# Where the short chunk of keys stands in a streamed cross attention: last instead of first

## Chip, core and metric

One Trainium2 core of one chip runs the whole program in one launch. The metric is the device time of that launch in microseconds (us); lower is better.

## The reference, cut to what matters

The program computes two layers of a Perceiver-like network on 128 queries of width 256, with a context of 12544 rows of width 256. The change touches the first block alone, a softmax attention of 16 heads (key width 64, value width 16) from the queries to the context:

```
q = layernorm(x) @ wq            # 128 x 1024, 16 heads of 64
k = ctx @ wk;  v = ctx @ wv      # 12544 x 1024, 12544 x 256
x = x + softmax(q k^T / 8) v     # per head, over all 12544 keys
```

The softmax runs over chunks of keys with a running maximum, so the result doesn't depend on the order of the chunks. A small attention, a gated feed-forward net, a second cross attention, another attention and a mixture of experts follow. They are not changed and wait for the first block's sum.

## The kernel before, in words

12544 keys are 24 chunks of 512 and one of 256 (`CHUNK_TILES` = 4 tiles of 128 keys, `TAIL_TILES` = 2). Two buffers ("slots") alternate for everything that a chunk owns. The five engines' programs are written out by hand and meet at semaphores; each engine works strictly in its own order.

A chunk has eight **steps** t, each with 32 queries of 8 heads. For a step TensorE (PE) forms scores (`scores`, L383), VectorE (DVE) takes the extreme over the keys (`maxima`, L604), ScalarE (ACT) takes exponentials from the score banks (`exponentials`, L541, two per step), and DVE transposes them (`turn_probabilities`, L623). Two pairs of score banks alternate, so PE's scores of step t+2 wait for ACT to have read step t (`scores_read`).

Between the scores PE makes the **keys of the next chunk** (`next_keys`, L360: 8 head pairs p, six matmuls each, since fp32 is split into high and low fp32r parts), this chunk's **values** (L367) and the sum **weighted** by the previous chunk's probabilities (L393). ACT copies the keys out (`keep_keys`, L531), some between the two exponentials of a step.

What depends on the running maximum goes a longer way. After step 7 ACT writes the factor `x_shrink` (L556, signal `alpha_ready`), SP places it per head with 16 small DMAs (`place_by_head`, L818), and GpSimd (POOL) then runs, in this order, `rescale` (L766 to L772), `set_aside` (L783, which prepares `vals`, the stationary side of the weighted sum, and signals `vals_ready`), `split_context` (L749) and `add_out` (L755, L758).

At the beginning the ACT queue loads the first chunk's context and then `wk` and `wv`; the SP queue loads `x`, `wq` and the second chunk's context at the same time. Before the first step there are the queries (L375), the split of `wk` into high (ACT, L568, L573) and low (DVE, L708) parts, and all eight key groups of the first chunk. At the end, `last_chunk` has no keys of a next chunk to make. It does the weighted sum of the chunk before in four quarters at t = 0 to 3, and its own in two parts: head quads (0, 1) after the scores of step 7 and once `vals_ready` is there, quads (2, 3) after the last transposition and after `acc_whole`, with small reordering matmuls (L449) between. Then come `outputs` and the next block.

Before, the order is 256, 512, ..., 512. Each full chunk's keys are always made in the chunk before.

Of the kernel before, what the change touches and what calls it, by code (L numbers as in the profile page):

```python
# [335 lines left out]
KEEP_BETWEEN, KEEP_AFTER = {0: 5, 4: 0}, {1: (6, 7), 5: (1, 2), 6: (3,), 7: (4,)}  # L336


def step_after(slot, t, nt, ahead, by=1):

    if t + by < STEPS:
        return slot, t + by, nt
    return (1 - slot, t + by - STEPS, CHUNK_TILES) if ahead else None


LAST_HALF, LAST_SUM = 3, 4
# [7 lines left out]
def xattn0_tensor(pe, m, s, n):  # L354
# [54 lines left out]
    def next_keys(slot, p, ahead):  # L409

        if p < 2:
            values_turned()
        if p == 0:
            pe.wait_ge(s["ctx_split"], n("ctx_split", 2))
            if ahead > 1:
                pe.sem_inc(s["raw_free"], 1)
        if p >= 2 and p != 5:
            pe.wait_ge(s["k_kept"], n("k_kept"))
        for i in range(TERMS):
            done = key_term(1 - slot, p, CHUNK_TILES, 4 + p % 2, i)  # L420
# [74 lines left out]
    for half in range(2):  # L495
        queries(half)
        if half == 0:
            pe.wait_ge(s["ctx_split"], n("ctx_split", 2))
            pe.sem_inc(s["raw_free"], 1)
        pe.wait_ge(s["wk_split"], n("wk_split"))  # L500
        for p in range(4 * half, 4 * half + 4):
            if p % 4 >= 2:
                pe.wait_ge(s["k_kept"], n("k_kept"))
            for i in range(TERMS):
                done = key_term(0, p, TAIL_TILES, 4 + p % 2, i)
            done.then_inc(s["k_full"], 1)
        pe.wait_ge(s["q_ready"], n("q_ready"))
        if half == 0:
            pe.wait_ge(s["k_kept"], n("k_kept", 2))
            for t in range(2):  # L510
                scores(0, t, TAIL_TILES)
    pe.wait_ge(s["wv_split"], n("wv_split"))
    chunk(0, TAIL_TILES, 0, 2)
    chunk(1, CHUNK_TILES, TAIL_TILES, 2)
    for _ in range((N_FULL - 4) // 2):
        chunk(0, CHUNK_TILES, CHUNK_TILES, 2)
        chunk(1, CHUNK_TILES, CHUNK_TILES, 2)
    chunk(0, CHUNK_TILES, CHUNK_TILES, 2)
    chunk(1, CHUNK_TILES, CHUNK_TILES, 1)
    last_chunk(0, CHUNK_TILES, CHUNK_TILES)  # L520


def xattn0_scalar(act, m, s, n):
    def split_context(slot, k, nt):
        if k == 0:
            act.wait_ge(s[f"raw{slot}"], n(f"raw{slot}", 16))
        act.copy(m.c_hi[slot][:, k, 0:nt * P], m.raw[slot][:, k, 0:nt * P]).then_inc(s["ctx_hi"], 1)  # L527

    def keep_keys(slot, p, nt):
        act.wait_ge(s["k_full"], n("k_full"))  # L530
        act.copy(m.keys[slot][:, p, 0:nt * P], m.bank(4 + p % 2)[:, 0:nt * P]).then_inc(s["k_kept"], 1)  # L531

    def keep_queries(half):
        act.wait_ge(s["q_full"], n("q_full"))
        act.mul(m.qT[:, 4 * half:4 * half + 4, :], m.bank(6 + half).rearrange("p (h c) -> p h c", c=P),
                -float(X0_DK) ** -0.5).then_inc(s["q_ready"], 1)

    def exponentials(slot, t, nt, between=None):
        act.wait_ge(s["max_ready"], n("max_ready"))
        for odd in range(2):  # L540
            i = act.activation(m.probs[t % 2][:, odd, 0:nt * P], m.ps[:, 2 * (t % 2) + odd, 0:nt * P], ACT.Exp,  # L541
                               bias=m.peak[slot][:, 1, 2 * (t // 4) + odd, t % 4:t % 4 + 1], scale=-1.0,
                               accum_out=m.totals[slot][:, 1, 2 * (t // 4) + odd, t % 4:t % 4 + 1])
            if odd == 0 and between:
                keep_keys(*between, CHUNK_TILES)
        i.then_inc(s["probs_ready"], 1)
        act.drain().then_inc(s["scores_read"], 1)  # L547

    def chunk(slot, nt, ahead, first=False):
        for t in range(2 if first else 0, STEPS):  # L550
            keys = 1 - slot if t > 1 else slot
            kept = t < 2 or ahead
            exponentials(slot, t, nt, (keys, KEEP_BETWEEN[t]) if kept and t in KEEP_BETWEEN else None)
            if t == STEPS - 1:
                act.wait_ge(s["below_ready"], n("below_ready"))
                act.activation(m.shrink[slot][:, :, :, :], m.below[:, :, :, :],  # L556
                               ACT.Exp).then_inc(s["alpha_ready" if ahead else "alpha_last"], 1)
            if kept:
                for p in KEEP_AFTER.get(t, ()):
                    keep_keys(keys, p, CHUNK_TILES)  # L560
            if ahead > 1 and t in SPLIT_STEPS:
                split_context(slot, SPLIT_STEPS.index(t), CHUNK_TILES)

    for k in range(DK):
        split_context(0, k, TAIL_TILES)
    layer_norm_scalar(act, m, s, n, 3)
    act.wait_ge(s["wk0"], 16)
# [25 lines left out]
    chunk(0, CHUNK_TILES, 2)  # L593
    chunk(1, CHUNK_TILES, 1)
    chunk(0, CHUNK_TILES, 0)
    act.wait_ge(s["last_full"], 1)
    act.copy(m.last_out[:, :, :], m.ps[:, 6:8, 0:P]).then_inc(s["last_kept"], 1)


def xattn0_vector(dv, m, s, n):  # L600
# [112 lines left out]
    maxima(0, 0, TAIL_TILES)  # L713
    chunk(0, TAIL_TILES, 0, 2)
    chunk(1, CHUNK_TILES, 1, 2)
    chunk(0, CHUNK_TILES, 2, 2)
    chunk(1, CHUNK_TILES, 2, 2)
# [5 lines left out]
        n.restart(dv, s, *looped)  # L723
    chunk(0, CHUNK_TILES, 2, 2)
    chunk(1, CHUNK_TILES, 2, 1)
    last_chunk(0, CHUNK_TILES)
    outputs()


def xattn0_pool_init(gp, m, s, n):  # L730
    for k in range(DK):
        gp.wait_ge(s["ctx_hi"], n("ctx_hi"))
        gp.tensor_tensor(m.c_lo[0][:, k, 0:TAIL], m.raw[0][:, k, 0:TAIL], m.c_hi[0][:, k, 0:TAIL],
                         ALU.subtract).then_inc(s["ctx_split"], 1)
    gp.memset(m.peak[0][:, 0, :, :], 3e38)
    gp.memset(m.totals[0][:, 0, :, :], 0.0)
# [9 lines left out]
def xattn0_pool(gp, m, s, n):  # L746
# [74 lines left out]
def xattn0_sync(sp, m, s, n, a):  # L821
# [973 lines left out]
```

## Time and profile before

| | us |
|---|---|
| median of 3 runs (lowest, highest) | 983.76 (981.04, 983.9) |
| the profiled execution: its own time | 983.17 |
| its span in the trace | 981.4 |
| PE busy in the span | 950.7 (97%) |
| end of the first cross attention in the span | about 657 |

The trace gives each instruction's start and duration. A matmul's recorded duration holds its latency, so the pace of a stream is read from the starts, or from the chain of waits, which gives a stretch and the number of instructions in it. A plain fp32 matmul of the program is recorded as two instructions: the eight score matmuls of one step are "x16". The program's line numbers in the rows are those of the listing above.

### The profile page before, as it was taken

Reading aid. Unit: us, or ns where it says so; the run is one execution under the profiler, and the core shown is the slowest. Engines: PE = TensorE matmul, PEld = TensorE weight load, DVE = VectorE, ACT = ScalarE, POOL = GpSimd, SP = SyncE. Lnnn points to the kernel's source line nnn. Section 1 sums busy time; section 2 is a strip of 40 time slices with the busy share of each in tenths; the row PEclk is TensorE's granted clock in tenths of the full one; section 3 lists DMA queues with packets and bytes.
Section 4 is the critical chain, followed back from the end, with each engine's and each line's share of the span. In section 5 each row is a group of like instructions: output and inputs, shape, how many; then the busy total and the mean of one; then the engine's idle time right before and its main releaser. Section 6 shows DMA issues by size and latency. Waiting matters only on the chain.

```text
span 981.4 us, 30783 instructions
## 1 busy us (share of the span) xinstructions
PE 950.7 (97%) x13281; PEld 702.9 (72%) x13281; DVE 692.2 (71%) x871; ACT 587.1 (60%) x1404; POOL 368.3 (38%) x405
## 2 busy tenths in 40 slices
PE   6999999999999999999999999988989999899998
PEld 6666666666666666666666666668977787789998
DVE  3788888888888888888888888763025555467886
ACT  5677766666666667666666666622236663336664
POOL 2344444444444444444444343330013333213332
PEclk9999999999999999999999999998999999999999
DMA  6010101000000000000100000049538888508993
GB/s 220 25 25 24 24 24 24 25 24 24 25 24 24 25 24 25 24 24 24 25 24 24 25 3 3 4 186 390 182 149 264 276 279 286 173 1 277 325 336 97
DMA packets 78295, 97.80 MB, mean 100 GB/s; under 512 B 21584, under 2 KB 56672, under 8 KB 78176
## 3 DMA queue, kind: packets, MB, share of 16 engines
q1 hardware_dynamic: 77088, 94.40, 29.7%
q8 instruction: 104, 1.70, 0.7%
q10 hardware_dynamic: 1088, 1.57, 0.4%
q14 instruction: 15, 0.12, 0.0%
HBM read 95.42 MB, written 0.13 MB: 97 GB/s over the span
## 4 chain that ended last, share of the span: by engine, by line
PE 89%; issue 4%; DVE 3%; POOL 2%; DMA 2%; ACT 1%; SPq 0%; ACTq 0%; DVEq 0%; POOLq 0%
PE ps L360 29%; PE ps L383 18%; PE ps L393 10%; PE ps L367 7%; PE ps L1493 6%; PE ps L1098 3%; PE ps L997 3%; PE ps L1510 2%; PE ps L1514 2%; PE ps L1511 2%; PE ps L1087 1%; PE ps L1089 1%; POOL m_w_lo L1475 1%; PE ps L1088 1%; DMA m_shared_w<-in_m_sw 1%
## 5 line engine op out<-in xcount | busy, mean ns | idle before, releaser
L541 ACT ACTIVATE probs<-ps,x_peak 128x512 f32<-128x512 f32 (+1 forms) x400 | 269.5, 678 | 178.1 <-DVE x_peak L604 167.4
L604 DVE TENSOR_REDUCE x_peak<-ps 128x2 f32<-128x1024 f32 (+1 forms) x200 | 237.0, 1185 | 93.7 <-PE ps L383 93.7
L623 DVE STREAM_TRANSPOSE probsT<-probs 128x1024 f32<-128x1024 f32 (+1 forms) x200 | 242.9, 1215 | 13.2 <-ACT probs L541 12.7
L383 PE MATMUL ps<-keys,qT 64*32 64x512 f32 (+1 forms) x3200 | 195.7, 584 | 2.5 <-ACTq L547 1.6
L360 PE MATMUL ps<-ctxT_hi,wk_hi 128*128 128x512 f32 (+1 forms) x400 | 163.2, 408 | 0.8 <-ACT keys L531 0.8
L360 PE MATMUL ps<-ctxT_lo,wk_hi 128*128 128x512 f32 (+1 forms) x400 | 155.2, 388 | 0.0
L783 POOL TENSOR_SCALAR vals<-vals_t,x_side 128x512 f32<-128x512 f32 (+1 forms) x100 | 152.2, 1541 | 7.6 <-PEq L407 3.9
L360 PE MATMUL ps<-ctxT_hi,wk_lo 128*128 128x512 f32 (+1 forms) x400 | 154.2, 386 | 0.0
L360 PEld LDWEIGHTS ps<-ctxT_hi,wk_hi 128*128 128x128 f32 x400 | 75.6, 189 | 73.7 <-issue 39.8
L531 ACT COPY keys<-ps 128x512 f32<-128x512 f32 (+1 forms) x200 | 110.4, 577 | 28.7 <-PE ps L360 20.8
L749 POOL TENSOR_TENSOR ctxT_lo<-ctx_raw,ctxT_hi 128x512 fp32r<-128x512 f32 x48 | 61.6, 1284 | 133.4 <-ACT ctxT_hi L527 133.4
L383 PEld LDWEIGHTS ps<-keys,qT 64*32 64x32 f32 x3200 | 58.7, 106 | 70.6 <-issue 52.5
L393 PE MATMUL ps<-probsT,vals 64*32 64x128 f32 x6272 | 104.2, 271 | 1.4 <-DVE probsT L623 1.4
L393 PEld LDWEIGHTS ps<-probsT,vals 64*32 64x32 f32 x6272 | 90.5, 105 | 19.7 <-issue 19.6
L360 PEld LDWEIGHTS ps<-ctxT_hi,wk_lo 128*128 128x128 f32 x400 | 75.6, 189 | 15.7
L360 PEld LDWEIGHTS ps<-ctxT_lo,wk_hi 128*128 128x128 f32 x400 | 75.8, 189 | 12.2
L541 ACT ACTIVATION_READ_ACCUMULATOR probs<-ps,x_peak 128x1 f32 x400 | 78.5, 196 | 0.0
L1279 POOL TENSOR_TENSOR c1T_lo<-ctx_two,c1T_hi 128x512 fp32r<-128x512 f32 (+1 forms) x25 | 31.3, 1251 | 103.7 <-ACT c1T_hi L1160 103.7
L766 POOL TENSOR_TENSOR x_parts<-x_totals,x_shrink 128x32 f32<-128x32 f32 x24 | 6.1, 253 | 159.5 <-DMA x_shrinkT<-x_shrink 159.5
L1465 POOL TENSOR_TENSOR m_w_lo<-m_w,m_w_hi 128x1024 fp32r<-128x1024 f32 x15 | 35.5, 2364 | 72.0 <-ACT m_w_hi L1542 72.0
L1493 PE MATMUL ps<-xnT,m_w 128*128 128x128 f32 x512 | 59.9, 275 | 0.0
L1493 PEld LDWEIGHTS ps<-xnT,m_w 128*128 128x128 f32 x512 | 58.6, 192 | 0.3 <-issue 0.3
(252 smaller groups left out, 1302.3 us busy)
## 6 DMA issues: line engine op xcount, KB each, us to landing
m_w<-in_m_w SPq DMA_DIRECT2D x32, 1024.0 KB, 7.7
ctx_raw<-in_ctxT SPq DMA_DIRECT2D x24, 512.0 KB, 3.7
ctx_two<-in_ctxT SPq DMA_DIRECT2D x24, 512.0 KB, 4.3
ctx_one<-in_ctx SPq DMA_DIRECT2D x24, 512.0 KB, 5.6
x_shrinkT<-x_shrink SPq DMA_DIRECT2D x384, 1.0 KB, 1.7
f_h1T<-in_f_h1T SPq DMA_DIRECT2D x1, 4096.0 KB, 18.2
f_h2T<-in_f_h2T SPq DMA_DIRECT2D x1, 4096.0 KB, 27.9
m_shared_w<-in_m_sw SPq DMA_DIRECT2D x2, 1024.0 KB, 7.9
```

The source lines that it names most:

```text
L360: return pe.matmul(m.bank(bank)[:, 0:nt * P], w[:, k, p * P:(p + 1) * P], c[:, k, 0:nt * P], start=(i == 0), stop=(i == TERMS - 1))
L367: return pe.matmul(m.bank(4 + half)[:, 0:nt * P], w[:, k, half * P:(half + 1) * P], c[:, k, 0:nt * P], start=(i == 0), stop=(i == TERMS - 1))
L383: i = pe.matmul(m.ps[32 * j:32 * (j + 1), 2 * (t % 2) + odd, 0:nt * P], m.qT[rows, 4 * group + j, qs], m.keys[slot][rows, 4 * group + j, 0 ...
L393: i = pe.matmul(m.ps[32 * c:32 * (c + 1), 6 + two, 0:P], m.vals[slot][rows, b, c, :], m.probsT[slot][rows, c, b, :], start=(b == 0), stop= ...
L531: act.copy(m.keys[slot][:, p, 0:nt * P], m.bank(4 + p % 2)[:, 0:nt * P]).then_inc(s["k_kept"], 1)
L541: i = act.activation(m.probs[t % 2][:, odd, 0:nt * P], m.ps[:, 2 * (t % 2) + odd, 0:nt * P], ACT.Exp, bias=m.peak[slot][:, 1, 2 * (t // 4) ...
L604: dv.tensor_reduce(m.peak[slot][:, 1, cs, t % 4], m.ps[:, 2 * (t % 2):2 * (t % 2) + 2, 0:nt * P], AX.X, ALU.min).then_inc(s["dve" if t == ...
L623: i = dv.transpose(m.probsT[slot][:, cs, 0:4 * nt, t % 4 * 32:t % 4 * 32 + 32], m.probs[t % 2][:, :, 0:nt * P].rearrange("p c (b k) -> p c ...
L749: gp.tensor_tensor(m.c_lo[slot][:, k, 0:nt * P], m.raw[slot][:, k, 0:nt * P], m.c_hi[slot][:, k, 0:nt * P], ALU.subtract).then_inc(s["ctx_ ...
L783: t = gp.tensor_scalar(m.vals[slot][:, 0:4 * nt, cs, side * X0_DV:(side + 1) * X0_DV], m.vals_t[slot][:, 0:4 * nt, cs, :], m.side[:, side: ...
L1465: eng.tensor_tensor(m.w2_lo[c % 2][:, os, :], second_weights(m, c)[:, os, :], m.w2_hi[c % 2][:, os, :], ALU.subtract).then_inc(s[f"m_w2_lo ...
L1493: t = pe.matmul(m.bank(2 * (c % 2) + half)[:, i * P:(i + 1) * P], w1[:, k, o * P:(o + 1) * P], m.xnT[:, k, :], start=(k == 0), stop=(k == ...
```

## The change

The tail of 256 keys becomes the last chunk and the first chunk has 512 keys. The tail's context is still the first 256 columns of the array; only the time of its turn changes. `following(ahead)` gives the size of the chunk whose keys are made ahead (256 when one chunk is left), and `third` the size of the context that is split two chunks ahead. Counts of instructions don't change on PE, DVE, ACT and POOL; the shapes at both ends do. The core of the diff:

```diff
+def following(ahead):
+    return TAIL_TILES if ahead == 1 else CHUNK_TILES
...
-            done = key_term(1 - slot, p, CHUNK_TILES, 4 + p % 2, i)
+            done = key_term(1 - slot, p, following(ahead), 4 + p % 2, i)
...
-                done = key_term(0, p, TAIL_TILES, 4 + p % 2, i)
+                done = key_term(0, p, CHUNK_TILES, 4 + p % 2, i)
...
-                scores(0, t, TAIL_TILES)
+                scores(0, t, CHUNK_TILES)
...
-    chunk(0, TAIL_TILES, 0, 2)
-    chunk(1, CHUNK_TILES, TAIL_TILES, 2)
+    chunk(0, CHUNK_TILES, 0, 2)
+    chunk(1, CHUNK_TILES, CHUNK_TILES, 2)
...
-    last_chunk(0, CHUNK_TILES, CHUNK_TILES)
+    last_chunk(0, TAIL_TILES, CHUNK_TILES)
...
-    chunk(0, CHUNK_TILES, 2, 2)
+    chunk(0, CHUNK_TILES, 2, 2, TAIL_TILES)
     chunk(1, CHUNK_TILES, 2, 1)
-    chunk(0, CHUNK_TILES, 2, 0)
+    chunk(0, TAIL_TILES, 2, 0)
...
-    act.dma_start(m.raw[0][:, :, 0:TAIL], columns[:, :, 0:TAIL]).then_inc(s["raw0"], 16)
+    act.dma_start(m.raw[0][:, :, :], columns[:, :, TAIL:TAIL + CHUNK]).then_inc(s["raw0"], 16)
```

ScalarE's program at the very beginning, before: `ctx_raw` is the context as loaded, `wk_hi` the high part of the key weights, `qT` the queries, `keys` the kept keys.

```order
L859 DMA ctx_raw_76<-in_ctxT 128x2x256
L862 DMA x_wk<-in_x_wk 128x2x512 x2
L863 DMA x_wv<-in_x_wv 128x2x256
L527 ACT_TABLE_LOAD
L527 CAST ctxT_hi_78<-ctx_raw_76 128x256 x2
L295 COPY xnT<-ps 128x256
L568 CAST wk_hi<-x_wk 128x2x512
L535 ACTIVATE qT<-ps 128x512
L531 COPY keys_69<-ps 128x256 x4
```

The same place of the changed kernel:

```order
L867 DMA ctx_raw_76<-in_ctxT 128x2x512
L870 DMA x_wk<-in_x_wk 128x2x512 x2
L871 DMA x_wv<-in_x_wv 128x2x256
L532 ACT_TABLE_LOAD
L532 CAST ctxT_hi_78<-ctx_raw_76 128x512 x2
L295 COPY xnT<-ps 128x256
L574 CAST wk_hi<-x_wk 128x2x512
L540 ACTIVATE qT<-ps 128x512
L536 COPY keys_69<-ps 128x512 x4
```

The order is the same; the first load is twice as large and stands ahead of `wk` in its queue, and the casts and copies have 512 columns.

TensorE in the last chunk before, from the second quarter of the weighted sum of the chunk before (`vals_87`) to the reordering; `vals_86` belongs to the last chunk:

```order
L393 MATMUL ps<-probsT_89,vals_87 32x128 x32
L383 MATMUL ps<-keys_69,qT 32x512 x8
L393 MATMUL ps<-probsT_89,vals_87 32x128 x32
L383 MATMUL ps<-keys_69,qT 32x512 x8
L393 MATMUL ps<-probsT_89,vals_87 32x128 x32
L383 MATMUL ps<-keys_69,qT 32x512 x16
L393 MATMUL ps<-probsT_88,vals_86 32x128 x64
L449 MATMUL ps<-acc,ident 32x64 x8
L393 MATMUL ps<-probsT_88,vals_86 32x128 x64
L449 MATMUL ps<-acc,ident 32x64 x8
```

And in the changed kernel:

```order
L398 MATMUL ps<-probsT_89,vals_87 32x128 x32
L388 MATMUL ps<-keys_69,qT 32x256 x8
L398 MATMUL ps<-probsT_89,vals_87 32x128 x32
L388 MATMUL ps<-keys_69,qT 32x256 x8
L398 MATMUL ps<-probsT_89,vals_87 32x128 x32
L388 MATMUL ps<-keys_69,qT 32x256 x16
L398 MATMUL ps<-probsT_88,vals_86 32x128 x32
L454 MATMUL ps<-acc,ident 32x64 x8
L398 MATMUL ps<-probsT_88,vals_86 32x128 x32
L454 MATMUL ps<-acc,ident 32x64 x8
```

The scores halve in width and the last chunk's weighted sum in number; the three quarters shown for the chunk before keep their full count.

## Rows read from the trace of the kernel before

**Rows 1.** The page's first part: busy us, share of the span, instructions.

```profile
PE 950.7 (97%) x13281; PEld 702.9 (72%) x13281; DVE 692.2 (71%) x871; ACT 587.1 (60%) x1404; POOL 368.3 (38%) x405
```

**Rows 2.** Chain of waits, first 70 us: start us, us, what.

```profile
20.62 1.70 PE ps L360 x12
...
26.72 4.35 PE ps L360 x18
31.07 1.02 PE ps L383 x32
...
35.03 1.88 PE ps L383 x32
...
43.09 2.94 PE ps L367 x12
46.03 1.09 PE ps L393 x64
```

**Rows 3.** Chain of waits, end of the first cross attention.

```profile
607.67 1.96 PE ps L393 x128
...
612.63 4.30 PE ps L360 x18
...
649.62 3.70 PE ps L393 x128
```

**Rows 4.** Timeline, loads and splits at the start: start, duration, engine, what [idle<-releaser].

```profile
8.11 1.04 ACT L568 CAST wk_hi<-x_wk 128x1024 fp32r<-128x1024 f32 x1 [1.36 <-DMA x_wk<-in_x_wk]
...
9.18 1.23 DVE L708 TENSOR_TENSOR wk_lo<-x_wk,wk_hi 128x1024 fp32r<-128x1024 f32 x1 [3.65 <-ACT wk_hi L568]
```

**Rows 5.** DMA queues from 7.05 to 8.11 us (q1 SP's, q10 ACT's).

```profile
q1 hardware_dynamic: 108, 0.22, 54.5%
q10 hardware_dynamic: 105, 0.21, 51.2%
```

**Rows 6.** Timeline, key matmuls of 256 columns around 12.9 us.

```profile
12.66 0.38 PE L360 MATMUL ps<-ctxT_hi,wk_hi 128*128 128x256 f32 x1
...
12.87 0.29 PE L360 MATMUL ps<-ctxT_lo,wk_hi 128*128 128x256 f32 x1
...
13.00 0.28 PE L360 MATMUL ps<-ctxT_hi,wk_lo 128*128 128x256 f32 x1
```

**Rows 7.** Timeline, key matmuls that waited for ACT [idle<-releaser].

```profile
20.62 0.39 PE L360 MATMUL ps<-ctxT_hi,wk_hi 128*128 128x256 f32 x1 [0.84 <-ACT keys L531]
```

**Rows 8.** Busy time by stretch: us, busy (x) of each engine, PEclk, DMA, GB/s.

```profile
10.50:12.66 2.16, 2.16 (x12) 2.16 (x11) 0.00 (x0) 0.97 (x2) 0.00 (x0) 1.00 1.06 381
```

**Rows 9.** Groups by line and form, first 660 us: busy us, mean ns | idle before.

```profile
L541 ACT ACTIVATE probs<-ps,x_peak 128x512 f32<-128x512 f32 x384 | 262.0, 686 | 174.7 <-DVE x_peak L604 164.2 <-DVEq L608 4.9 <-issue 0.4
L623 DVE STREAM_TRANSPOSE probsT<-probs 128x1024 f32<-128x1024 f32 x192 | 237.3, 1236 | 11.2 <-ACT probs L541 10.7
L604 DVE TENSOR_REDUCE x_peak<-ps 128x2 f32<-128x1024 f32 x192 | 231.7, 1207 | 89.4 <-PE ps L383 89.4
```

**Rows 10.** Timeline, POOL's `set_aside` of the first (256) chunk.

```profile
26.28 3.64 POOL L783 TENSOR_SCALAR vals<-vals_t,x_side 128x256 f32<-128x256 f32 x4 [0.41 <-PEq L407]
```

**Rows 11.** Timeline of the end: factor, placement, POOL's part.

```profile
621.64 0.69 ACT L541 ACTIVATE probs<-ps,x_peak 128x512 f32<-128x512 f32 x1 [0.17 <-DVEq L608]
...
623.20 0.23 ACT L556 ACTIVATE x_shrink<-x_below 128x32 f32<-128x32 f32 x1
...
635.89 0.25 POOL L766 TENSOR_TENSOR x_parts<-x_totals,x_shrink 128x32 f32<-128x32 f32 x1 [6.44 <-DMA x_shrinkT<-x_shrink]
...
636.97 0.22 POOL L772 TENSOR_TENSOR x_totals<-x_parts 128x16 f32<-128x16 f32 x1
637.51 6.18 POOL L783 TENSOR_SCALAR vals<-vals_t,x_side 128x512 f32<-128x512 f32 x4 [0.32 <-PEq L407]
...
647.85 0.34 PE L449 MATMUL ps<-acc,ident 32*32 32x64 f32 x16
```

**Rows 12.** Waits after 650 us: the only one on a transfer.

```profile
POOL m_w_hi L1473 <- DMA m_shared_w<-in_m_sw: 2.1, 1, 2.1
```

More of the change, by code:

```diff
@@ L342, in step_after @@
         return slot, t + by, nt
-    return (1 - slot, t + by - STEPS, CHUNK_TILES) if ahead else None
+    return (1 - slot, t + by - STEPS, following(ahead)) if ahead else None
 LAST_HALF, LAST_SUM = 3, 4
@@ L544, in exponentials, with chunk @@
             if odd == 0 and between:
-                keep_keys(*between, CHUNK_TILES)
+                keep_keys(*between)
         i.then_inc(s["probs_ready"], 1)
         act.drain().then_inc(s["scores_read"], 1)
-    def chunk(slot, nt, ahead, first=False):
+    def chunk(slot, nt, ahead, first=False, third=CHUNK_TILES):
         for t in range(2 if first else 0, STEPS):
-            keys = 1 - slot if t > 1 else slot
+            keys, tiles = (1 - slot, following(ahead)) if t > 1 else (slot, nt)
             kept = t < 2 or ahead
-            exponentials(slot, t, nt, (keys, KEEP_BETWEEN[t]) if kept and t in KEEP_BETWEEN else None)
+            exponentials(slot, t, nt, (keys, KEEP_BETWEEN[t], tiles) if kept and t in KEEP_BETWEEN else None)
             if t == STEPS - 1:
@@ L559, in chunk @@
                 for p in KEEP_AFTER.get(t, ()):
-                    keep_keys(keys, p, CHUNK_TILES)
+                    keep_keys(keys, p, tiles)
             if ahead > 1 and t in SPLIT_STEPS:
-                split_context(slot, SPLIT_STEPS.index(t), CHUNK_TILES)
+                split_context(slot, SPLIT_STEPS.index(t), third)
     for k in range(DK):
-        split_context(0, k, TAIL_TILES)
+        split_context(0, k, CHUNK_TILES)
     layer_norm_scalar(act, m, s, n, 3)
@@ L570, in xattn0_scalar @@
     for p in range(4):
-        keep_keys(0, p, TAIL_TILES)
+        keep_keys(0, p, CHUNK_TILES)
     act.wait_ge(s["wk1"], 16)
@@ L575, in xattn0_scalar @@
     act.copy(m.wv_hi[:, :, :], m.wv[:, :, :]).then_inc(s["wv_hi"], 1)
-    exponentials(0, 0, TAIL_TILES)
+    exponentials(0, 0, CHUNK_TILES)
     keep_queries(1)
     for p in range(4, 6):
-        keep_keys(0, p, TAIL_TILES)
-    exponentials(0, 1, TAIL_TILES)
+        keep_keys(0, p, CHUNK_TILES)
+    exponentials(0, 1, CHUNK_TILES)
     for p in range(6, 8):
-        keep_keys(0, p, TAIL_TILES)
+        keep_keys(0, p, CHUNK_TILES)
     for k in range(DK):
         split_context(1, k, CHUNK_TILES)
-    chunk(0, TAIL_TILES, 2, first=True)
+    chunk(0, CHUNK_TILES, 2, first=True)
     chunk(1, CHUNK_TILES, 2)
@@ L592, in xattn0_scalar @@
         n.restart(act, s, *looped)
-    chunk(0, CHUNK_TILES, 2)
+    chunk(0, CHUNK_TILES, 2, third=TAIL_TILES)
     chunk(1, CHUNK_TILES, 1)
-    chunk(0, CHUNK_TILES, 0)
+    chunk(0, TAIL_TILES, 0)
     act.wait_ge(s["last_full"], 1)
@@ L712, in xattn0_vector @@
     dv.wait_ge(s["x0_init"], 1)
-    maxima(0, 0, TAIL_TILES)
-    chunk(0, TAIL_TILES, 0, 2)
+    maxima(0, 0, CHUNK_TILES)
+    chunk(0, CHUNK_TILES, 0, 2)
     chunk(1, CHUNK_TILES, 1, 2)
@@ L725, in xattn0_vector @@
     chunk(1, CHUNK_TILES, 2, 1)
-    last_chunk(0, CHUNK_TILES)
+    last_chunk(0, TAIL_TILES)
     outputs()
@@ L732, in xattn0_pool_init @@
         gp.wait_ge(s["ctx_hi"], n("ctx_hi"))
[L733 removed]
+        gp.tensor_tensor(m.c_lo[0][:, k, :], m.raw[0][:, k, :], m.c_hi[0][:, k, :],
                          ALU.subtract).then_inc(s["ctx_split"], 1)
@@ L785, in set_aside, with chunk @@
         t.then_inc(s["vals_ready"], 1)
-    def chunk(slot, nt, order, ahead):
+    def chunk(slot, nt, order, ahead, third=CHUNK_TILES):
         if order >= 1:
@@ L792, in chunk @@
             for k in range(DK):
-                split_context(slot, k, CHUNK_TILES)
+                split_context(slot, k, third)
         if order >= 1:
@@ L798, in xattn0_pool @@
         split_context(1, k, CHUNK_TILES)
-    chunk(0, TAIL_TILES, 0, 2)
+    chunk(0, CHUNK_TILES, 0, 2)
     chunk(1, CHUNK_TILES, 1, 2)
@@ L827, in xattn0_sync @@
     sp.dma_start(m.wq[:, :, BANK:2 * BANK], wq[:, :, BANK:2 * BANK]).then_inc(s["wq1"], 16)
-    sp.dma_start(m.raw[1][:, :, :], full[0]).then_inc(s["raw1"], 16)
+    sp.dma_start(m.raw[1][:, :, :], full[1]).then_inc(s["raw1"], 16)
     sp.wait_ge(s["raw_free"], n("raw_free"))
-    sp.dma_start(m.raw[0][:, :, :], full[1]).then_inc(s["raw0"], 16)
+    sp.dma_start(m.raw[0][:, :, :], full[2]).then_inc(s["raw0"], 16)
     sp.dma_start(m.a0_wqT[:, :, :], a["a0_wqT"].rearrange("(k p) n -> p k n", p=P)).then_inc(s["a0_weights"], 16)
@@ L836, in xattn0_sync, with chunk @@
     sp.dma_start(m.s3[:, :], a["f_w3_s"].partition_broadcast(P)).then_inc(s["f_scale"], 16)
-    def chunk(slot, src):
+    def chunk(slot, src, size=CHUNK):
         if src is not None:
             sp.wait_ge(s["raw_free"], n("raw_free"))
-            sp.dma_start(m.raw[1 - slot][:, :, :], src).then_inc(s[f"raw{1 - slot}"], 16)
+            sp.dma_start(m.raw[1 - slot][:, :, 0:size], src).then_inc(s[f"raw{1 - slot}"], 16)
         sp.wait_ge(s["alpha_ready"], n("alpha_ready"))
         place_by_head(sp, m.shrinkT[slot], m.shrink[slot], s[f"alpha_placed{slot}"])
-    chunk(0, full[2])
-    chunk(1, full[3])
+    chunk(0, full[3])
+    chunk(1, full[4])
     n.restart(sp, s, "raw_free", "alpha_ready")
-    with sp.Fori(0, (N_FULL - 4) // 2) as i:
-        chunk(0, full[i * 2 + 4])
-        chunk(1, full[i * 2 + 5])
+    with sp.Fori(0, (N_FULL - 6) // 2) as i:
+        chunk(0, full[i * 2 + 5])
+        chunk(1, full[i * 2 + 6])
         n.restart(sp, s, "raw_free", "alpha_ready")
+    chunk(0, full[N_FULL - 1])
+    chunk(1, columns[:, :, 0:TAIL], TAIL)
     for slot in range(2):
```

## The prediction, made before the changed kernel was run

> **What bounds the kernel now.** I read the page's first part, then the chain of waits at both ends of the first cross attention, then the timeline around every place where the chain leaves TensorE. PE is busy 97% of the span [rows 1], and in the steady part the chain is nothing but PE: keys, scores, values, weighted sum in turn [rows 2, 3]. So the work on PE, which the change only carries from one end to the other, can't matter by itself. What matters is how much of it is paid at each end. At the start some of it may fall into gaps; at the end PE waits for others, so not all that is taken away comes back. The answer is a difference of two numbers of 10 us or more, and I work out each.
>
> **The cost at the start: PE's extra work.** The prices are the pace at either width. Twelve matmuls (keys or values) take 1.70 us at 256 columns and 2.94 at 512, so 1.24 for twelve. Two steps of scores take 1.02 and 1.88, so 0.86 for two [rows 2]. Half a weighted sum takes 1.09 us for a 256 chunk and 1.96 for a 512 chunk, so 0.87 more [rows 2, 3].
> - Keys of the first chunk: 48 matmuls, 4 x 1.24 = 5.0 us.
> - Values: 12 matmuls, 1.2 us.
> - Scores: 8 steps, 4 x 0.86 = 3.4 us.
> - Its weighted sum, in the chunk after: 2 x 0.87 = 1.7 us.
> Together 11.4 us.
>
> **The cost at the start: loads and waits.** The first load is 256 KB larger and stands before `wk` in ACT's queue. From 7.05 to 8.11 us SP's queue moved 0.22 MB and ACT's 0.21 MB [rows 5]: each has half, some 0.2 MB a microsecond. So 0.26 MB more in ACT's queue is 1.3 us for `wk`, while `wq` in the other queue comes when it did. If both queues shared the delay at their joint 0.4 MB/us it would be 0.65 us; that is the lower end. ACT's `wk_hi` was released by that transfer at 8.11 and DVE's `wk_lo` by `wk_hi` [rows 4], and the first keys need `wk_lo`, and `wk_lo` ended at 10.41; the queries on PE cover 0.1 of it, so they start 1.2 us later. That is +1.2.
>
> The Trainium skill bears on this ("DMA: Bandwidth & Descriptors", Queues, rings and completion order): each DMA engine takes turns, packet by packet, between the queues that have work for it. This trace agrees, by the 0.22 and 0.21 MB. By that rule alone the delay is the 1.3 us taken; it adds nothing to the sum.
>
> The first key matmuls run at the slower pace. They start 0.21 us apart up to 12.87 and 0.13 apart from there, which for 256 columns are the levels of 1.2 and 2.4 GHz [rows 6], though the granted clock is given as 1.00 [rows 8]. PE had the queries before that. If it rises at the same moment, the keys that now start 1.2 us later meet 1.2 us less of the slow stretch, and half of that is lost work: -0.6. If it waits for a new unbroken stretch, this term is +0.6.
>
> Gaps of before that the wider work fills: key group 6 waited 0.84 us for ACT, which was still at exponentials [rows 7]. In the changed kernel ACT has two groups of 2.94 us in which to do that, so it goes; with a few tenths around it, -1.0. New waits: a full step asks DVE for 1.21 + 1.24 us and ACT for 2 x (0.69 + 0.2) [rows 9], and in the first chunk no weighted sum lies beside it. Two steps on PE without one are 1.88 + 2.94 = 4.82 us, on DVE 4.89. By going through the steps one by one I find two places where PE waits about 0.5 us for a score bank, against one of 0.5 before: +0.5. The start: 11.4 + 1.2 - 0.6 - 1.0 + 0.5 = **+11.5 us**, between 10.3 and 13.
>
> **What comes back at the end.** The first gain is in the last full chunk, where the keys made ahead are the tail's. The three groups that took 4.30 us [rows 3] take 2.3 (18 x 0.12 and the first one's 0.2). The scores of step 6 start 2.0 us earlier, at 614.9. DVE is free for them at 615.9, and from there maxima and exponentials follow in order, so ACT's first exponential of step 7, released by DVE at 621.64 [rows 11], comes at 619.7, and the factor is written at 621.5 and not 623.43. Later key groups save more on PE, but this chain no longer sees it.
>
> From the factor on there is a chain that knows nothing of the chunk's size. POOL's L766 came at 635.89, so 12.46 us after the factor, because SP places it with 16 transfers one after the other. Before, this was hidden: `set_aside` ended at 643.7 [rows 11], about when PE had its last scores. Now:
> - factor 621.5 + 12.46 = 633.9, POOL begins;
> - `rescale`, 635.89 to 637.19, 1.3 us: 635.2; 0.2 to the next;
> - `set_aside` of a 256 chunk 3.64 us [rows 10]: `vals_ready` at 639.05;
> - weighted sum of quads (0, 1): 128 records took 3.70 us at this end [rows 3], 64 take 1.85: 640.9;
> - reordering 0.34 [rows 11]: 641.25; quads (2, 3) 1.85: 643.1.
> Before, this point was 649.62 + 3.70 = 653.3 [rows 3]. So the end gives back **10.2 us**.
>
> Is PE or DVE later than 639.05? Scores of the tail begin about 620.9. There are scores 8 x 0.5, values 2 x 0.75, three key groups 2.2, the sum of the chunk before in quarters, 4 x 1.1, and some 2.5 of waits for ACT, which puts the last scores at 634.7. Two exponentials and two short transpositions are 3 us more: 637.7. So PE stands idle for about 4 us before `vals_ready`, and this stall is what a cut of 13.7 loses to become 10.2.
>
> After this point everything waits for the sum and moves with it. The weights of the feed-forward net are loaded on a signal given just before the last weighted sum, and that lead shrinks by 1.85 us. After 650 us only one wait ends on a transfer, 2.1 us on POOL, far from there [rows 12]; cost nothing. If that cover were gone it would cost at most those 1.85 us. The middle, 22 full chunks, is unchanged.
>
> **Sum.** +11.5 - 10.2 = +1.3 us on the profiled execution: 983.17 + 1.3 = **984.5 us** (its span 981.4 lies 1.8 below its time; the median of the three runs is 983.76, 0.6 above it). A measurement of this kernel tells a difference of about 0.3% from none, which is 2.95 us, so this is no measurable change.
>
> **Rivals.**
> *The first chunk turns DVE-bound (slower).* The pair without weighted sum is 4.82 us on PE and 4.89 on DVE, which turns the values and joins the maxima besides. If the score banks come back late at all four pairs and not at two, 0.5 to 0.8 each, and the clock rises late (+1.2 against my term), the start costs 11.5 + 1.3 + 1.2 = 14.0: 983.17 + 14.0 - 10.2 = 987.0 us. For it: there is little slack. Against it: three key groups fill two of the four pairs (6.2 us on PE). It decides from 1.7 us over my start on.
> *POOL's chain doesn't hold the end (faster).* If the placement takes less than 11.1 us (621.5 + 11.1 + 1.3 + 0.2 + 3.64 = 637.7), or POOL's times, which the trace gives roughly, are shorter, DVE's last transposition at 637.7 ends it: two parts of 1.85 and 0.34 behind or beside it, at best 639.6, so 13.7 back. With the start at its lower end of 10.3: 983.17 + 10.3 - 13.7 = 979.8 us; with mine 981.0. Against it: the placement took 12.46 us, and 1.4 would have to go.
> *The program moves little because the sizes don't change.* The order of the instructions excludes it: the shapes at both ends are exchanged as the change says.
>
> **Chances.** No measurable change, as forecast, 0.62. Slower by over 0.3% 0.23: the first rival, and unknown stalls at the start. Faster by over 0.3% 0.15: the second rival with a cheap start. The range takes the start from 10.3 to 13 and what comes back from 9.5 to 12.5, not all at once, and reaches to the rivals: 980.5 to 987.5 us.
>
> **What would show it.** `wk_lo` ending at about 11.7 us and not 10.4, and the key matmuls right behind it. PE's keys of the second chunk's last three groups at about 46.7 and not 36.9, and 1.7 us more lag in the chunk after: a lag of 11.5 in the steady part. POOL's L783 of the last chunk about 3.6 us long and ending just before PE's last weighted sums, with PE idle some 4 us ahead of them. DVE's last transposition before that. The distance from the last placed factor to the end of the sum about 9 us. I am wrong if the lag in the steady part is over 13 or under 10, or if PE doesn't wait for `vals` at the end.

## The result, and the profile after

| | us |
|---|---|
| before, beside it on the same chip | 982.75 median (980.39 to 984.32, 17 runs) |
| changed kernel | 985.69 median (982.61 to 987.35, 17 runs) |
| ratio | 1.0025, 95% interval 1.0016 to 1.0034 |
| span of the profiled execution | 984.4 (before 981.4) |

The changed kernel is 0.25% slower. That is inside the band called "no measurable change", 1.2 us above the forecast, and the interval excludes 1. As a difference of the two kernels it is +2.5 us by the ratio, where +1.3 was forecast. Line numbers of the changed kernel are five to eight higher: keys L365, scores L388, weighted sum L398, reordering L454, `set_aside` L789.

First the start. The timeline of the changed kernel shows what released the first keys (start, duration, operation, in brackets the idle time before and its end; PEld is the weight load):

```profile
8.78 1.04 ACT L574 CAST wk_hi<-x_wk 128x1024 fp32r<-128x1024 f32 x1 [2.21 <-DMA x_wk<-in_x_wk]
9.85 1.23 DVE L714 TENSOR_TENSOR wk_lo<-x_wk,wk_hi 128x1024 fp32r<-128x1024 f32 x1 [4.50 <-ACT wk_hi L574]
11.13 0.19 PEld L365 LDWEIGHTS ps<-ctxT_hi,wk_hi 128*128 128x128 f32 x1 [0.19 <-DVE wk_lo L714]
11.13 0.50 PE L365 MATMUL ps<-ctxT_hi,wk_hi 128*128 128x512 f32 x1
```

`wk_hi` came 0.67 us later than in [rows 4], and not 1.3. That is one profile of each kernel, and the start varies from one execution to the next: over four profiles with either start (those of the experiments are among them) `wk_hi` began at 7.54 to 8.11 us before and at 8.78 to 9.00 after. The first chunk's chain (start, us, what):

```profile
21.57 5.59 PE ps L365 x24
27.16 1.10 PE ps L388 x16
...
28.28 1.23 DVE x_peak L610
29.51 1.15 DVE probsT L629
30.66 1.12 DVE x_peak L610
...
31.80 0.69 ACT probs L546
32.49 0.80 ACTq L552
...
33.34 1.09 PE ps L388 x16
```

Four key groups run in one piece, so the wait for ACT of [rows 7] is gone. After the scores of 27.16 the chain leaves PE for the maxima on DVE, and comes back at 33.34. The same happens once more, before the scores at 44.97. These are the two score-bank waits that were forecast; PE itself stood idle for 0.34 us before 33.34 and 0.40 us before 44.97. The last full chunk, whose keys made ahead are the tail's:

```profile
609.31 4.33 PE ps L365 x18
613.64 1.88 PE ps L388 x32
615.52 2.94 PE ps L372 x12
618.46 1.96 PE ps L398 x128
620.42 1.63 PE ps L388 x22
622.05 0.35 issue
622.41 1.07 PE ps L388 x10
623.48 2.35 PE ps L365 x18
```

Three groups take 2.35 us and not 4.30. They stand at 623.48, where [rows 3] had 612.63: a lag of 10.85 us. Now the end of the chain:

```profile
646.92 0.67 PE ps L388 x16
647.59 2.84 issue
650.43 3.64 PE ps L398 x64
654.06 0.39 PE ps L454 x16
654.46 2.66 PE ps L398 x64
```

PE waits 2.84 us behind its last scores, and then 64 weighted matmuls take 3.64 us, where 128 took 3.70 [rows 3]. The windows tell why (columns: busy us and instructions of PE, PEld, DVE, ACT and POOL, granted clock, DMA share, GB/s):

```profile
647.00:648.00 1.00, 0.59 (x16) 0.11 (x16) 1.00 (x3) 0.66 (x3) 1.00 (x2) 1.00 0.00 0
648.00:649.00 1.00, 0.00 (x0) 0.00 (x0) 0.85 (x2) 0.77 (x4) 1.00 (x2) 1.00 0.00 0
649.00:650.00 1.00, 0.00 (x0) 0.00 (x0) 0.97 (x4) 0.84 (x5) 1.00 (x2) 0.60 0.00 0
650.00:651.00 1.00, 0.57 (x12) 0.60 (x16) 0.93 (x4) 0.00 (x0) 0.87 (x3) 0.50 0.00 0
655.00:656.00 1.00, 1.00 (x28) 0.90 (x21) 0.00 (x0) 0.00 (x0) 0.00 (x0) 0.50 0.89 78
656.00:657.00 1.00, 1.00 (x40) 0.84 (x32) 0.00 (x0) 0.00 (x0) 0.00 (x0) 0.98 0.96 360
```

While PE waited the granted clock fell from 1.00 to 0.50, so from 2.4 to 1.2 GHz, and it was back only when the weighted sum was nearly over. Before, it was 1.00 all through this place, also behind the 1.43 us in which PE waited for DVE there:

```profile
648.00:649.60 1.60, 0.19 (x16) 0.04 (x6) 1.56 (x4) 0.42 (x3) 0.00 (x0) 1.00 0.00 0
649.60:653.30 3.70, 3.68 (x131) 3.50 (x134) 0.63 (x3) 0.00 (x0) 0.00 (x0) 1.00 0.61 213
```

What held PE is on POOL:

```profile
645.21 0.25 POOL L772 TENSOR_TENSOR x_parts<-x_totals,x_shrink 128x32 f32<-128x32 f32 x1 [9.14 <-DMA x_shrinkT<-x_shrink]
646.28 0.22 POOL L778 TENSOR_TENSOR x_totals<-x_parts 128x16 f32<-128x16 f32 x1
646.71 3.62 POOL L789 TENSOR_SCALAR vals<-vals_t,x_side 128x256 f32<-128x256 f32 x4 [0.21 <-POOL x_totals L778]
```

`vals` was ready at 646.71 + 3.62 = 650.33, and PE began at 650.43. The last DVE operation of the block:

```profile
659.43 0.43 DVE L706 TENSOR_TENSOR x_odd<-x_y,x_y_last 128x256 f32<-128x256 f32 x1
```

It ended at 659.86. The same operation of the kernel before, in its chain of waits, ended at 657.28:

```profile
656.85 0.43 DVE x_odd L700
```

So the block ends 2.6 us later, and of the 10.85 us of lag 8.3 came back and not 10.2.

### The profile page after: what moved, and what is told of

Same layout as the page of the kernel before. It is cut to its first block, busy times and chain, and to the rows that moved or that the text cites. A ratio compares the mean times of both kernels' runs of the same rounds, so it can differ in the third digit from the quotient of the medians.

```text
span 984.4 us, 30774 instructions
## 1 busy us (share of the span) xinstructions
PE 951.5 (97%) x13281; PEld 702.3 (71%) x13281; DVE 690.3 (70%) x871; ACT 587.2 (60%) x1404; POOL 368.5 (37%) x405
## 4 chain that ended last, share of the span: by engine, by line
PE 88%; issue 4%; DVE 3%; POOL 2%; DMA 2%; ACT 1%; SPq 0%; ACTq 0%; DVEq 0%; POOLq 0%
PE ps L365 28%; PE ps L388 18%; PE ps L398 10%; PE ps L372 7%; PE ps L1501 6%; PE ps L1106 3%; PE ps L1005 3%; PE ps L1518 2%; PE ps L1522 2%; PE ps L1519 2%; PE ps L1095 1%; DMA m_shared_w<-in_m_sw 1%; POOL m_w_lo L1483 1%; PE ps L1097 1%; PE ps L1096 1%
## 5 line engine op out<-in xcount | busy, mean ns | idle before, releaser
L629 DVE STREAM_TRANSPOSE probsT<-probs 128x1024 f32<-128x1024 f32 (+1 forms) x200 | 242.9, 1215 | 10.3 <-ACT probs L546 9.3
L388 PE MATMUL ps<-keys,qT 64*32 64x512 f32 (+1 forms) x3200 | 195.8, 584 | 4.5 <-ACTq L552 1.9
L365 PE MATMUL ps<-ctxT_hi,wk_hi 128*128 128x512 f32 (+1 forms) x400 | 162.6, 407 | 0.0
L789 POOL TENSOR_SCALAR vals<-vals_t,x_side 128x512 f32<-128x512 f32 (+1 forms) x100 | 152.1, 1540 | 9.5 <-PEq L412 5.2
L365 PE MATMUL ps<-ctxT_lo,wk_hi 128*128 128x512 f32 (+1 forms) x400 | 154.7, 387 | 0.0
L365 PE MATMUL ps<-ctxT_hi,wk_lo 128*128 128x512 f32 (+1 forms) x400 | 153.9, 385 | 0.0
L365 PEld LDWEIGHTS ps<-ctxT_hi,wk_hi 128*128 128x128 f32 x400 | 74.9, 187 | 73.4 <-issue 39.8
L755 POOL TENSOR_TENSOR ctxT_lo<-ctx_raw,ctxT_hi 128x512 fp32r<-128x512 f32 (+1 forms) x48 | 60.4, 1260 | 138.4 <-ACT ctxT_hi L532 138.3
L388 PEld LDWEIGHTS ps<-keys,qT 64*32 64x32 f32 x3200 | 58.5, 106 | 73.8 <-issue 55.3
L398 PE MATMUL ps<-probsT,vals 64*32 64x128 f32 x6272 | 104.8, 274 | 2.8 <-issue 2.8
L398 PEld LDWEIGHTS ps<-probsT,vals 64*32 64x32 f32 x6272 | 90.7, 106 | 19.9 <-issue 19.3
L365 PEld LDWEIGHTS ps<-ctxT_hi,wk_lo 128*128 128x128 f32 x400 | 75.2, 188 | 15.7
L365 PEld LDWEIGHTS ps<-ctxT_lo,wk_hi 128*128 128x128 f32 x400 | 75.3, 188 | 12.4
```

What stands on the lines that cost most here:

```text
L365: return pe.matmul(m.bank(bank)[:, 0:nt * P], w[:, k, p * P:(p + 1) * P], c[:, k, 0:nt * P], start=(i == 0), stop=(i == TERMS - 1))
L388: i = pe.matmul(m.ps[32 * j:32 * (j + 1), 2 * (t % 2) + odd, 0:nt * P], m.qT[rows, 4 * group + j, qs], m.keys[slot][rows, 4 * group + j, 0 ...
L398: i = pe.matmul(m.ps[32 * c:32 * (c + 1), 6 + two, 0:P], m.vals[slot][rows, b, c, :], m.probsT[slot][rows, c, b, :], start=(b == 0), stop= ...
L629: i = dv.transpose(m.probsT[slot][:, cs, 0:4 * nt, t % 4 * 32:t % 4 * 32 + 32], m.probs[t % 2][:, :, 0:nt * P].rearrange("p c (b k) -> p c ...
L755: gp.tensor_tensor(m.c_lo[slot][:, k, 0:nt * P], m.raw[slot][:, k, 0:nt * P], m.c_hi[slot][:, k, 0:nt * P], ALU.subtract).then_inc(s["ctx_ ...
L789: t = gp.tensor_scalar(m.vals[slot][:, 0:4 * nt, cs, side * X0_DV:(side + 1) * X0_DV], m.vals_t[slot][:, 0:4 * nt, cs, :], m.side[:, side: ...
```

## Experiments

Theory A: the forecast misses what PE's clock does. The stall before `vals_ready` costs its own 2.84 us and then some 2.6 us at half clock. The rivals were that the slow weighted sum belongs to the short chunk's thin work, and that the start with its loads is what costs. Each batch had its own runs of the kernel before: median 982.16 us (27 runs) for the kernels with ten spare products, with POOL's new order (two) and with the split load, 983.09 us (29 runs) for the other three. A ratio below is to the runs of the kernel before in the same batch.

**Ten spare products in the stall.** They multiply the identity into a bank that isn't in use. The helper (L280) is already in the kernel before, which calls it at six places, but not in this stall.

```diff
+            if t == 5:
+                spare_products(pe, m, 5, 10)
             if t in (0, 5):
```

> The changed kernel, with ten spare matmul products (20 records, about 2.3 us at full clock) on TensorE in the last chunk between the scores of step 7 and the wait for vals_ready, where it stood idle 2.84 us. Theory A (the granted clock fell to 0.50 because of that idle time, and the weighted sums of quads (0,1) and (2,3), 3.64 and 2.66 us, ran at half pace): the clock stays at 1.00 there, both parts take about 1.85 us, vals_ready stays where it is, and the kernel is 2.6 us faster than the changed one, so level with the one before (within 1 us). Rival B (64 records in two parts have a fixed cost, the clock has nothing to do with it): both parts stay at about 3.6 and 2.7 us and the time doesn't move.

Measured: 983.80 us (11 runs), 1.0011 of before (1.0002 to 1.002). PE's timeline:

```profile
646.60 0.67 PE L388 MATMUL ps<-keys,qT 64*32 64x256 f32 x16 [0.58 <-ACTq L554]
647.19 2.50 PE L283 MATMUL ps<-ident 128*128 128x128 f32 x20
650.64 2.30 PE L398 MATMUL ps<-probsT,vals 64*32 64x128 f32 x64 [0.95 <-issue]
652.88 0.34 PE L454 MATMUL ps<-acc,ident 32*32 32x64 f32 x16
653.15 1.95 PE L398 MATMUL ps<-probsT,vals 64*32 64x128 f32 x64
```

`vals` was ready no earlier, the clock stayed at 1.00, and 2.30 and 1.95 us stand for 3.64 and 2.73. The block ended at 657.9, so 2.0 us earlier; from `vals` ready to that point it took 7.3 us and not 9.5. A is right here in what it says of the clock. Its 2.6 us were not all given back: the first part keeps 0.4 us over its full pace, and the kernel is 1.1 us over the one before by the ratio, just outside the 1 us allowed.

**Five spare products**, the same line with 5 for 10.

> The changed kernel with five spare products (10 records, about 1.2 us) in the stall before vals_ready and not ten: about 2.2 us of the stall stay empty. If what counts is whether the idle stretch is broken up early, the clock stays at 1.00 and the block ends at 657.9 as with ten; if it is the length of the empty piece next to the weighted sum, the clock falls and the block ends between 658.5 and 659.9, the first weighted part taking 3 us or more. Time of the whole: 983.8 by the first, 984.8 to 985.7 by the second.

Measured: 983.79 us (12 runs), 1.0008 (0.9997 to 1.0018):

```profile
647.35 1.38 PE L283 MATMUL ps<-ident 128*128 128x128 f32 x10
650.24 1.95 PE L398 MATMUL ps<-probsT,vals 64*32 64x128 f32 x64 [1.51 <-issue]
652.39 1.95 PE L398 MATMUL ps<-probsT,vals 64*32 64x128 f32 x64
```

The clock stayed at 1.00, as in the first answer. PE was empty for 1.51 us next to the weighted sum, and not for the 2.2 expected, so the run doesn't tell whether it matters that the stall was broken up early or only that the rest of it was short. From the start of the last scores to the end of the block it took 10.3 us (646.76 to 657.09) against 12.9 in the changed kernel: here the 2.6 us are given back in full.

**The same stall in the kernel before.** If the clock is the cause, the kernel before must show it when it is made to wait. In the last chunk each of POOL's four operations on `vals` gets a second one ahead of it, on half as many tiles, which writes what is written over right behind it. (`n` counts the signal, so the wait is a constant.)

```diff
+                if again:
+                    gp.tensor_scalar(m.vals[slot][:, 0:2 * nt, cs, ...], ...).then_inc(s["pool"], 1)
+                    gp.wait_ge(s["pool"], n("pool"))
                 t = gp.tensor_scalar(m.vals[slot][:, 0:4 * nt, cs, ...
```

> The kernel before, with four more GpSimd operations on 128x256 elements (0.93 us each, and a wait behind each) inside the last chunk's preparation of vals, so that vals_ready comes about 4.1 us later, at 647.8 and not 643.7. They write what is written over right behind them. TensorE then stands idle for 3.4 us after its last scores (1.43 us at another place before). Theory A (a stall of about 3 us at the end is itself followed by a stretch at half clock, in whatever kernel): the first weighted part, 3.67 us for 128 records before, takes 5 us or more, PEclk shows about 0.5 behind the stall, and the block ends 2.4 us later by the wait and some 2.6 more by the clock, at about 662.3 where before it was 657.3. Rival (the half clock of the changed kernel belongs to the short chunk's thin work and not to the stall): 3.7 us, PEclk 1.00, the block ends at 659.7. By the time of the whole: +5 against +2.4 us.

Measured: 985.75 us (11 runs), 1.0029 (1.0017 to 1.0041). PE's timeline and windows of it:

```profile
642.29 1.09 PE L383 MATMUL ps<-keys,qT 64*32 64x512 f32 x16 [1.12 <-ACTq L547]
647.10 5.57 PE L393 MATMUL ps<-probsT,vals 64*32 64x128 f32 x128 [3.72 <-issue]
```

```profile
644.00:646.00 2.00, 0.00 (x0) 0.00 (x0) 1.85 (x3) 1.13 (x5) 1.91 (x3) 0.54 0.00 0
650.00:651.00 1.00, 1.00 (x28) 1.00 (x24) 0.00 (x0) 0.00 (x0) 0.00 (x0) 0.50 0.00 0
651.00:652.00 1.00, 1.00 (x44) 1.00 (x40) 0.00 (x0) 0.00 (x0) 0.00 (x0) 1.00 0.00 0
```

The full-size sum, 3.67 us before, takes 5.57 with the clock at 0.50 up to 651. So the short chunk isn't needed for it: the rival, 3.7 us at a clock of 1.00, is out. A gave "5 us or more"; the loss is 1.9 us and not 2.6, because the clock was back sooner, 3.9 us after PE had begun again (5.6 us in the changed kernel). In the sum A was too high: it had the block end at 662.3 and the whole +5 us, and they were 660.04 and +2.9 us by the ratio. Part of both costs fell into a wait that the kernel before has anyway: its 1.43 us for DVE ahead of the second part are gone here. And its stall of 0.96 us within the reordering, of unknown cause, is 0.48 here.

**That kernel with twelve spare products in the stall.**

> As the run before it, and twelve spare products with the identity on TensorE (20 records took 2.4 us elsewhere, so 24 take about 2.9) in the stall. Theory A: PEclk stays 1.00, the first weighted part takes about 3.7 us, the block ends near 660 (+2.4 to +3 against the kernel before), so 2 us or more before the run without them. Rival: the spare products change nothing, both end at the same time.

Measured: 984.24 us (11 runs), 1.0013 (1.0001 to 1.0025):

```profile
643.78 2.94 PE L283 MATMUL ps<-ident 128*128 128x128 f32 x24
647.58 4.09 PE L393 MATMUL ps<-probsT,vals 64*32 64x128 f32 x128 [0.85 <-issue]
```

The first weighted part is 1.5 us shorter, at PEclk 1.00, and by the medians the kernel is 1.5 us faster than without the products; expected were 2 or more. The rival, that they change nothing, is out. The block ended at 659.55, only 0.5 us sooner: this execution began 0.45 us later (its last full chunk's 18 key matmuls at 612.34 and not 611.89), and its second part holds a stall of 0.86 us marked "issue". As in the first run, the part behind the spare products is 0.4 us longer than at full pace; why isn't known.

**POOL prepares `vals` first.** This takes the wait itself away: `set_aside` doesn't need the placed factors, it only stands behind `rescale`, which does.

```diff
+        if ahead == 0:
+            set_aside(slot, nt)
         if order >= 1:
             rescale(1 - slot)
-        set_aside(slot, nt)
+        if ahead:
+            set_aside(slot, nt)
```

> The changed kernel; on GpSimd, in the last chunk alone, set_aside (which prepares vals) runs before rescale (which waits for the placed factor). Theory A (the end is held by the chain factor, placement 12.9 us, rescale 1.3, set_aside 3.6): vals_ready comes about 5 us earlier (645.3 for 650.3 in the changed kernel's own frame), TensorE has no long idle time before its last weighted sums, the clock stays up, and DVE's last transposition (650.4) becomes the bound: the end of the block 4 to 5 us earlier, so about 981 us against 985.7, and 1 to 2.5 us faster than the kernel before. Rival C (TensorE, ACT and DVE are as late anyway): under 1 us gained.

Measured: 980.64 us (11 runs), 0.9992 of before (0.9981 to 1.0002). POOL and PE:

```profile
641.87 1.82 POOL L789 TENSOR_SCALAR vals<-vals_t,x_side 128x256 f32<-128x256 f32 x2 [5.02 <-PEq L412]
644.67 1.82 POOL L789 TENSOR_SCALAR vals<-vals_t,x_side 128x256 f32<-128x256 f32 x2 [0.98 <-PEq L412]
646.46 0.25 POOL L772 TENSOR_TENSOR x_parts<-x_totals,x_shrink 128x32 f32<-128x32 f32 x1
```

```profile
647.48 2.09 PE L398 MATMUL ps<-probsT,vals 64*32 64x128 f32 x64
650.92 1.95 PE L398 MATMUL ps<-probsT,vals 64*32 64x128 f32 x64 [0.96 <-DVE probsT L629]
```

The stall and the half clock are both gone, and DVE's last transposition (ended 650.78) bounds the end, as the prediction's second rival would have had it. The block ends at 655.6, 4.2 us before the changed kernel's. `vals` was ready at 646.49 and not at the expected 645.3, since its second half waited for PE's signal. This is the fastest version. Against the kernel before it is not told apart from no change; 1 to 2.5 us had been expected.

**The same order of POOL in the kernel before**, as a control.

> Control: the same reordering of set_aside and rescale in the last chunk, on the kernel before (the short chunk first). Theory A: there set_aside was ready before TensorE could use it and DVE's last transposition bounds the end; the values were turned only 0.3 us after rescale had ended, so nothing can be gained: within 1 us of the kernel before. Rival D (the order of POOL's work costs time whatever the size of the last chunk): 2 us or more gained here too.

Measured: 983.28 us (11 runs), 1.001 (0.9997 to 1.0022): no gain. `set_aside` waited for `vals_turned` and began at 636.73, 0.8 us earlier than before, but that execution was 0.8 us ahead all along (611.86 for 612.63), and PE still waited 1.43 us for DVE. So what the order of POOL is worth hangs on the short last chunk.

**Half of the first load moved to the other queue**, so that `wk` comes as it did before.

```diff
     sp.dma_start(m.x[0][:, :], a["x"]).then_inc(s["x"], 16)
+    sp.dma_start(m.raw[0][:, :, TAIL:CHUNK], columns[:, :, 2 * TAIL:TAIL + CHUNK]).then_inc(s["raw0"], 16)
     sp.dma_start(m.wq[:, :, 0:BANK], wq[:, :, 0:BANK]).then_inc(s["wq0"], 16)
...
-    act.dma_start(m.raw[0][:, :, :], columns[:, :, TAIL:TAIL + CHUNK]).then_inc(s["raw0"], 16)
+    act.dma_start(m.raw[0][:, :, 0:TAIL], columns[:, :, TAIL:2 * TAIL]).then_inc(s["raw0"], 16)
```

> The changed kernel; of the first chunk's context the second half (256 columns, 256 KB) is loaded by SP's queue right behind x, and ACT's queue has 256 KB ahead of wk as in the kernel before. Theory A (both queues share one delay, since wk_hi started 0.67 us later in the changed kernel and the first query matmul 0.30 later): wk_hi starts about as late as in the changed kernel (8.8 us, within 0.3) because the total is the same, wq comes 0.3 to 0.6 us later, and the time doesn't change (within 1 us). Rival E (the queues have fixed halves and the load in front of wk costs by itself): wk_hi starts at about 8.1 us and the keys of the first chunk 0.5 us earlier.

Measured: 986.46 us (5 runs), 1.0046 (1.0033 to 1.006). Its first query:

```profile
9.52 3.75 PE L380 MATMUL ps<-xnT,x_wq 128*128 128x128 f32 x16 [3.46 <-DMA x_wq<-in_x_wq]
```

`wk_hi` came at 8.20, 0.6 to 0.8 us earlier than in the four profiles with the other start and not within 0.3 us as expected; that is the rival's figure (8.1). The queries came at 9.52, where those four have 7.32 to 7.61. So the expectation that the time would stay was wrong: the 256 KB cost 1.9 to 2.2 us in front of `wq`, and the first keys had to wait for PE, not for `wk_lo`. The steady lag grew to 13.9 us (626.51 for 623.48, from 612.63). Of the 3.0 us more, 2.0 are the queries, and 0.8 are the first 24 key matmuls, which ran at the slower pace up to 15.2 us here (6.51 us and not 5.74). The stall at the end was 3.54 us, with a clock of 0.50 behind it as well.

**All executions, and not only the profiled ones.** There is one trace of each kernel, but the mean granted clock was recorded for every execution. It was 0.991 or less in 12 of the 17 of the changed kernel and in 6 of the 11 of the kernel before with the late `vals`. It was so in 1 of 11 with ten spare products, 0 of 12 with five, 1 of 11 with twelve, 2 of 11 with `vals` first in the changed kernel, 0 of 11 with it first in the other, and in 6 of the 56 of the kernel before. So the fall isn't a chance of one execution. The mean isn't a sharp test, since it holds the later stages too: the profile with the split load has 0.995 in spite of its fall here, and its kernel 1 of 5. The five executions of the changed kernel with a higher mean took 982.61 to 985.21 us, the other twelve 984.74 to 987.35; whether the clock stayed up at this place in those five, no trace shows.

## Why the prediction was right, and where it wasn't

The forecast lay in its range and the path was the right one: a start some 11 us dearer, an end held by POOL's chain, PE idle ahead of `vals`. That the number came so near is in part luck. One term of 2.6 us was missing, and a start that was 0.65 us cheaper in this pair and a stall that the kernel before has at its end, which nobody had counted, made up for 1.7 of it. By the steps:

- *Start, +11.5 us.* Measured +10.85 between the two profiles. Over the profiles of kernels with the same start it is 10.9 to 12.4, 11.7 between the means of four and four (the 18 key matmuls of the last full chunk stand at 611.86 to 612.63 with the old start and at 623.48 to 624.27 with the new one). Right within that scatter; the 10.85 is its low end.
- *`wk` +1.2.* Too dear. Between the two profiles `wk_hi` was 0.67 us late and the first keys 0.5, which looks like the prediction's lower end (0.65, both queues share the delay), and the queries moved too, from 7.19 to 7.49. But between the means of the four profiles with either start `wk_hi` was 1.1 us late, near the 1.3 forecast, the queries 0.3, and the first keys 0.7. What failed is the "0.1": in the old start the keys came 0.19 to 0.71 us behind `wk_lo`, since PE was still at the queries, so the queries cover more of the delay. And "each has half" was read from 7.05 to 8.11 us alone: between 3 and 5 us SP's queue and ACT's moved 0.40 and 0.28 MB before, and 0.26 and 0.46 after.
- *Clock at the start, -0.6.* The changed kernel ran at full pace from its first keys. Of the four profiles with its start one was slow up to 13.2 us: 24 key matmuls took 6.65 us there and 5.74 in the changed kernel's. The moment varies from one execution to the next by more than the term.
- *Gap -1.0, new waits +0.5.* Both seen: the 0.84 us went, and there are two waits for a score bank, 0.34 and 0.40 us, where one of 0.48 was. A wait for ACT's keys before the first scores grew from 0.56 to 0.77. That is -0.4 in sum, where -0.5 was forecast.
- *The last full chunk's advance of 1.9 us on the factor.* ACT wrote it at 632.32, and 10.85 - (632.32 - 623.43) = 1.96. Right.
- *Placement 12.46 us.* It took 645.21 - 632.32 = 12.89. `rescale` and `set_aside` were as forecast.
- *PE idle some 4 us.* `vals` ended the wait, as forecast, but it was 2.84 us. The terms given for the last scores add up to 635.5 and not to the 634.7 written, so it should have said 3.5. And PE stood 1.52 us as "issue" inside the scores of step 5, which nobody had forecast; that 2.84 and 1.52 come near 4 is chance. DVE's last transposition ended at 650.45, 0.1 us behind `vals` and not 1.3 before it. PE needs it for the second part alone, so it cost nothing, but it is the next bound.
- *"64 take 1.85".* The step that failed, and the largest error. The two parts took 3.64 and 2.66 us, 2.6 more than 2 x 1.85, because the granted clock fell in the stall that the prediction itself had forecast. The Trainium skill has the rule ("TensorE: Matmul & The Clock Gate", Part 1: an idle stretch between bursts of matmuls puts TensorE back to its half clock; its example has longer stretches than this one). The trace agrees, with 0.50 from 650 on, behind only 2.84 us; I had used the clock for the start alone.
- *-10.2 in all.* By the steps: 10.2 less 2.6 for the clock and 0.4 for the placement is 7.2. At PE's last weighted matmul it is 7.05 (657.12 for 653.32, so 3.8 of the 10.85 are left); at the end of the block it is 8.3. The 1.1 between 7.2 and 8.3 is mostly a stall of 0.96 us within the reordering of the kernel before, marked "issue", that the changed kernel doesn't have. That stall falls where the next weights load at 406 GB/s, comes in other kernels too (0.86 and 0.48 us in the two with the late `vals`) and is missing in others with the same load (ten and five spare products, `vals` first in either kernel). Its cause stays open, and so does that of the stalls of 0.9 to 1.5 us in step 5's scores.

The sum by measured terms: +10.85 - 8.3 = +2.6 at the end of the block, +3.0 in the span. The other 0.4 lies in later stages that nothing of the change reaches, and is within their scatter: from the end of the block to the end of the span it was 322.7 to 324.5 us over the nine profiles.

## What to carry to other kernels

Where work is carried from a place in which the bounding engine is full to one in which it waits, write down the chain that becomes the bound there, and price the stall twice: its own length, and what TensorE loses behind it at half clock. Then look whether the waiting operation needs everything that stands before it on its engine. Here `set_aside` didn't need the factors. Moving it was worth 3.2 us by the ratios to the kernel before, 4.2 at the end of the block in the profiles and 5.0 by the medians, which come from different batches; five spare products in the stall, some 1.4 us of work, were worth 1.7 by the ratios and 1.9 by the medians. And look at what waits behind the stall. In the kernel before, `vals` was some 4 us later in its own course, and that cost 2.9 us with the fall of the clock and 1.3 without, since a later wait for DVE took up a part.

## What the runs showed of the hardware

- An idle PE of 2.84, 3.54 and 3.72 us at this end of the block was each time followed by a granted clock of 0.50, and PE's work on the weighted sum ran at about half pace for some 5.6, 3.4 and 3.9 us. The fall came at no fixed moment: some 1.6, 3.8 and 0.8 us after the last scores, in the second of these when PE had already begun again. Idle pieces of 0.85, 0.95 and 1.51 us behind spare products, of 1.43 and 1.12 us in the kernel before, and of 1.52 us in the changed kernel's step 5 left it at 1.00.
- The length of a gap is not all that counts. In the next stage, which the change doesn't touch, the clock fell too. In the kernel before it read 0.56 from 675.0 to 675.5 us, beside idle pieces of 0.81 and 0.46 us. In the changed kernel it read 0.52 from 676.5 to 677.0, within a run of matmuls of 17 columns, in which the trace shows no idle of PE from 672.2 to 677.9. What decides it is not shown here. What is shown is that with the stall partly filled by spare products the clock stayed up, in three kernels.
- Two queues that load at once don't always have half each: in the changed kernel 0.46 and 0.26 MB from 3 to 5 us, 0.39 and 0.37 MB from 5 to 7. In front of `wk` 256 KB delayed `wk_hi` by 0.67 to 1.46 us, 1.1 between the means of four profiles and four, and PE's queries in the other queue by 0.3; in front of `wq`, in that other queue, they cost the queries 1.9 to 2.2 us.
- The granted clock in the profile read 1.00 in stretches at the start in which the key matmuls ran at about half pace: 256 columns started 0.21 us apart and not 0.12, 512 columns 0.43 and not 0.23. The spacing of the starts tells it, and the column doesn't.
